# Expert results added in a PSUM bank, row shifts on ScalarE, and expert scatters through two tables

## What is computed

```python
h = h + _L0_attn_ref(_layernorm(h), ...)   # a state-space block with a scan over time
h = h + _L0_ffn_ref(_layernorm(h), ...)    # 8 experts, each takes the 1024 tokens of highest share
h = h + _L1_attn_ref(_layernorm(h), ...)   # windows of 64 tokens; per token, attention among 8 heads
h = h + _L1_ffn_ref(_layernorm(h), ...)    # shared expert + 2 of 8 experts per token, by group
```

```python
output = jnp.zeros_like(x_flat).at[idx.reshape(-1)].add(weighted.reshape(-1, Dd))
```

## Time and profile before

| what | value |
|---|---|
| three runs, median (lowest, highest) | 2762.41 us (2756.27, 2762.47) |
| the profiled execution's own time | 2761.4 us |
| its span, first to last instruction | 2759.4 us |
| VectorE busy | 2382.7 us (86%) |
| TensorE busy | 2294.0 us (83%) |
| GpSimd busy | 2068.2 us (75%) |
| ScalarE busy | 1616.4 us (59%) |

### The profile page before, as it was taken

The page is one execution under the profiler, slowest core; times in us unless marked ns, Lnnn a source line. Parts: engine busy times, 40 slices in busy tenths (PEclk is TensorE's granted clock), DMA queues, the critical chain, the costliest instruction groups (busy, mean ns, idle before and its releaser), DMA issues. The chain is left out here.

```text
span 2759.4 us, 26470 instructions
## 1 busy us (share of the span) xinstructions
PE 2294.0 (83%) x6899; PEld 1098.8 (40%) x6899; DVE 2382.7 (86%) x3555; ACT 1616.4 (59%) x3023; POOL 2068.2 (75%) x1108
## 2 busy tenths in 40 slices
PE   5999999999999999999984148717888888888888
PEld 2444444444444444444432024304444444444444
DVE  3999999999999999999996832226999999999996
ACT  4777777767777777777662124424545555555544
POOL 2889899898898898988992048766777777777772
PEclk8999999999999999999996569857999999999999
DMA  2243333333433333333333013311111111011100
GB/s 75 94 124 99 106 115 105 114 111 93 128 98 108 118 106 110 116 93 115 108 96 98 0 35 73 47 25 31 31 29 30 29 28 31 28 31 31 31 24 23
DMA packets 180609, 199.44 MB, mean 72 GB/s; under 512 B 40062, under 2 KB 170988, under 8 KB 180332
## 3 DMA queue, kind: packets, MB, share of 16 engines
q1 hardware_dynamic: 169196, 189.35, 22.5%
q0 software_dynamic: 11264, 8.40, 2.3%
HBM read 164.44 MB, written 33.25 MB: 72 GB/s over the span
## 5 line engine op out<-in xcount | busy, mean ns | idle before, releaser
L915 POOL TENSOR_TENSOR a_hc<-a_h,a_cs 128x896 f32<-128x896 f32 (+1 forms) x448 | 859.6, 1938 | 55.4 <-DVE a_h L778 54.9
L362 PE MATMUL a_y_bank<-a_hc,a_ident 128*128 128x448 f32 (+1 forms) x1792 | 741.4, 544 | 20.3 <-DVE a_yz L798 19.7
L553 ACT ACTIVATE a_da<-a_dt,a_neg_a 128x448 f32<-128x448 f32 (+1 forms) x896 | 551.8, 631 | 295.6 <-DVE a_h L778 290.6
L778 DVE TENSOR_TENSOR_SCAN a_h<-a_da,a_h,a_dbx 128x448 f32<-128x448 f32 x528 | 583.3, 1135 | 9.5 <-ACT a_da L553 4.4
L362 PEld LDWEIGHTS a_y_bank<-a_hc,a_ident 128*128 128x128 f32 x1792 | 331.6, 190 | 325.2 <-issue 273.0
L2183 POOL TENSOR_TENSOR c_prod<-c_prob,c_qkv 128x1024 f32<-128x1024 f32 x100 | 279.3, 2820 | 189.3 <-DVE c_prob L2053 189.3
L1777 PE MATMUL c_p_E<-c_w_ex,c_hid 128*128 128x512 f32 x800 | 375.4, 599 | 38.3 <-DVE c_sc L2029 36.3
L762 DVE TENSOR_TENSOR a_dbx<-a_dtx,a_b_bank 128x896 f32<-128x896 f32 (+1 forms) x308 | 327.8, 1064 | 15.7 <-PE a_b_bank L355 15.5
L2174 POOL TENSOR_TENSOR c_prod<-c_qkv 128x1024 f32<-128x1024 f32 x100 | 232.7, 2353 | 58.1 <-ACT c_qkv L1845 58.1
L903 POOL TENSOR_TENSOR a_dbp<-a_dtx,a_bs 128x896 f32<-128x896 f32 (+1 forms) x140 | 270.9, 1935 | 0.0
L778 DVE TENSOR_TENSOR_SCAN a_h<-a_da,a_h,a_dbp 128x448 f32<-128x448 f32 x240 | 263.4, 1130 | 0.0
(11 more groups left out here) (306 smaller groups left out, 3744.1 us busy)
## 6 DMA issues: line engine op xcount, KB each, us to landing
a_cs<-c_rows SPq DMA_DIRECT2D x96, 896.0 KB, 5.3
a_bs<-c_rows SPq DMA_DIRECT2D x24, 1120.0 KB, 5.7
a_cs<-c_rows SPq DMA_DIRECT2D x16, 900.0 KB, 4.4
c_x<-h_rows SPq DMA_DIRECT2D x100, 64.0 KB, 2.3
heads<-c_ot SPq DMA_DIRECT2D x25, 256.0 KB, 2.0
c_dealt<-heads SPq DMA_DIRECT2D x200, 32.0 KB, 1.9
rolled<-c_res SPq DMA_DIRECT2D x25, 256.0 KB, 2.4
h_rows<-a_th SPq DMA_DIRECT2D x24, 224.0 KB
```

What stands on the lines that cost most here:

```text
L362: pe.matmul(y_bank[:, d, 0:g.w], ident[:], hc[:, (g.i * NS + n) % HC_RING, d, 0:g.w], start=(n == 0), stop=(n == NS - 1)).then_inc(s_sum, 1)
L553: act.activation(da[:, k % DA_RING, 0:g.w], dt[g.slot][:, d, 0:g.w], ACT.Exp, scale=neg_a[:, d * NS + n:d * NS + n + 1]).then_inc(s_da, 1)
L778: dve.tensor_tensor_scan(h[:, n, d, 0:g.w], da[:, (g.i * 2 * NS + k) % DA_RING, 0:g.w], x, state, ALU.mult, ALU.add).then_inc(s_scan, 1)
L915: pool.tensor_tensor(hc[:, (q.i * NS + n) % HC_RING, :, 0:q.w], h[:, n, :, 0:q.w], cs[:, n % C_RING, 0:q.w].unsqueeze(1).to_broadcast([P, ...
```

## The change

1. Stage C: the experts' parts are no longer summed by two reductions over six slots. VectorE adds them one after another into the shared expert's PSUM bank: `total(c, 0)` adds the attention's rows `h3` to ACC, `total(c, 1)` to `(c, 3)` add a part of 128x512, and `total(c, 4)` writes the result. `keep_acc` goes.
2. The shift of both norms (minus mean times 1/deviation) is computed by ScalarE in four single-column copies behind `rstd`; `less_mean` and `less_mean2` go from VectorE.
3. Banks 1 and 2 of the experts are evicted by VectorE, `by_dve(1)` and `by_dve(2)`, instead of ScalarE.
4. Stage B: there are two tables of rows twice as wide, the norm in the first half and the running sum in the second. Even experts gather and scatter whole rows of table 0, odd ones of table 1, with plain scatters; the addition is done by VectorE in the gathered tile. The second table is filled in stage B: a copy of the norm, and zeros. A gather waits for the scatters of the expert two before.
5. Stage C loads a group from both tables, and GpSimd adds them (`merge`), on which `stats_of` waits.
6. Stage B's TensorE takes the halves of an expert in turn: transposes of a half, then its up-projection.
7. The order of the operations in a turn of stage C is another on all engines.

```diff
 # GpSimd, experts
-        for e in range(XG - 1):
-            gather(e)
+        for e in range(2):
+            gather(e)
         for e in range(E0):
-            if e + XG - 1 < E0:
-                gather(e + XG - 1)
             scatter(e)
+            if e + 2 < E0:
+                gather(e + 2)
...
+            if e == 1:
+                pool.wait_ge(s_second, 16 * SECOND)
+            if e >= 2:
+                pool.wait_ge(s_scatter, 16 * TILES * (e - 1))
...
-                pool.indirect_dma_start(h_rows[:, :], bass.IndirectOffsetOnAxis(ap=index[:, i, e:e + 1], axis=0),
-                                        og[e % 2][:, i, :], None, compute_op=ALU.add).then_inc(s_scatter, 16)
+                pool.indirect_dma_start(tables[e % 2][:, :], bass.IndirectOffsetOnAxis(ap=index[:, i, e:e + 1], axis=0),
+                                        xg[e % XG][:, i, :], None).then_inc(s_scatter, 16)
...
+                    last = dve.scalar_tensor_tensor(out=total, in0=p_t[h][:, i * P:(i + 1) * P], scalar=share[s][:, t:t + 1],
+                                                    in1=total, op0=ALU.mult, op1=ALU.add)
...
+        for b in range(BATCH):
+            span = slice(b * ROWS // BATCH, (b + 1) * ROWS // BATCH)
+            sp.dma_start(tables[1][span, 0:D], tables[0][span, 0:D]).then_inc(s_second, 16)
+        sp.wait_ge(s_fill, 2)
+        for top in range(0, ROWS, P * NZERO):
+            n = min(P * NZERO, ROWS - top)
+            per = NZERO if n == P * NZERO else n // 32
+            sp.dma_start(tables[1][top:top + n, D:2 * D].rearrange("(p k) d -> p k d", k=per),
+                         zeros[0:n // per, 0:per * D].bitcast(F32).rearrange("p (k d) -> p k d", k=per)
+                         ).then_inc(s_second, 16)
```

```diff
 # GpSimd, a turn of stage C
+            def merge():
+                if L is not None:
+                    pool.wait_ge(s_x[L % 3], (L // 3 + 1) * 16 * GT)
+                    pool.wait_ge(s_x2[L % 2], (L // 2 + 1) * 16 * GT)
+                    pool.tensor_tensor(x[L % 3][:], x[L % 3][:], x2[L % 2][:], ALU.add).then_inc(s_merged, 1)
...
             score_products(2)
+            score_products(3)
+            merge()
             add_experts(0)
-            score_products(3)
+            add_experts(1)
             value_products(0)
             value_products(1)
-            add_experts(1)
             add_experts(2)
 # VectorE
         def total(c, k):
+            acc = tile_of("acc", c)[:].rearrange("p (j d) -> p j d", j=GT)
+            if k == 0:
+                result(dve, "acc", c)
+                dve.tensor_tensor(acc, acc, h3[c % SUM_RING][:], ALU.add).then_inc(s_sum, 1)
+                return
+            dve.wait_ge(s_add, c * GT + GT)
+            dve.wait_ge(s_sum, c * EG + k)
+            part = parts[c % 2][:, :, k - 1, :]
+            if k < EG:
+                dve.tensor_tensor(acc, acc, part, ALU.add).then_inc(s_sum, 1)
+                return
...
+            dve.tensor_tensor(res[c % 2][:], acc, part, ALU.add).then_inc(s_free[nth["acc", c][0]], 1)
...
-                    dve.wait_ge(s_x[L % 3], (L // 3 + 1) * 16 * GT)
+                    dve.wait_ge(s_merged, L + 1)
```

More of the change, by code:

```diff
@@ L100, in dram @@
             return debug[name] if name in debug else nc.dram_tensor(name, shape, dt, kind="Internal").ap()
-        h_rows = dram("h_rows", [ROWS, D])
-        n_rows = dram("n_rows", [ROWS, D])
+        tables = [dram(f"rows{k}", [ROWS, 2 * D]) for k in range(2)]
+        n_rows, h_rows = tables[0][:, 0:D], tables[0][:, D:2 * D]
         logits = dram("logits", [E0, NLG])
@@ L1055, in phase_b @@
     w2 = [sb(f"w2{s}", [P, FT, D]) for s in range(2)]
-    xg = [sb(f"xg{s}", [P, TILES, D]) for s in range(XG)]
+    xg = [sb(f"xg{s}", [P, TILES, 2 * D]) for s in range(XG)]
     xw = [sb(f"xw{h}", [P, HT, D]) for h in range(2)]
@@ L1277, in vector @@
             dve.wait_ge(s_share, e + 1)
-            need(dve, s_scatter, 16 * TILES * (e - 1))
             for h in range(2):
                 dve.wait_ge(s_turned, 2 * e + h + 1)
-                dve.tensor_tensor(og[s][:, h * HT:(h + 1) * HT, :], p_t[h][:].rearrange("p (i d) -> p i d", i=HT),
-                                  share[s][:, h * HT:(h + 1) * HT].unsqueeze(2).to_broadcast([P, HT, D]), ALU.mult
-                                  ).then_inc(s_og, 1)
+                for i in range(HT):
+                    t = h * HT + i
+                    total = xg[e % XG][:, t, D:2 * D]
+                    last = dve.scalar_tensor_tensor(out=total, in0=p_t[h][:, i * P:(i + 1) * P], scalar=share[s][:, t:t + 1],
+                                                    in1=total, op0=ALU.mult, op1=ALU.add)
+                last.then_inc(s_og, 1)
     def scalar(act):
@@ L1576, in phase_c @@
     sc = sb("sc", [P, SC_RING, E1, D])
-    parts = [sb(f"parts{s}", [P, GT, SLOTS, D]) for s in range(SUM_RING)]
+    parts = [sb(f"parts{s}", [P, GT, EG, D]) for s in range(2)]
+    h3 = [sb(f"h3{s}", [P, GT, D]) for s in range(SUM_RING)]
     res = [sb(f"res{s}", [P, GT, D]) for s in range(2)]
@@ L1610, in phase_c @@
     s_x = [sem(f"x{s}") for s in range(3)]
+    s_x2 = [sem(f"x2{s}") for s in range(2)]
+    s_merged = sem("merged")
     s_heads, s_dealt, s_res = ([sem(f"{n}{s}") for s in range(2)] for n in ("heads", "dealt", "res"))
@@ L1654, in load @@
                         taken(sp, "proj", L - 3)
[L1655 to L1658, removed]
+                    need(sp, s_merged, L - 1)
+                    for table, tile, done in ((tables[0], x[L % 3], s_x[L % 3]), (tables[1], x2[L % 2], s_x2[L % 2])):
+                        rows = table[L * GW + SHIFT:(L + 1) * GW + SHIFT, D:2 * D].rearrange("(w n) d -> n w d", n=WIN)
+                        for j in range(GT):
+                            sp.dma_start(tile[:, j, :], rows[j * WIN // GT:(j + 1) * WIN // GT]).then_inc(done, 16)
             def store(c):
                 if c is not None and c >= 0:
-                    sp.wait_ge(s_sum, 2 * c + 2)
+                    taken(sp, "acc", c)
                     sp.dma_start(out[c * GW:(c + 1) * GW, :].rearrange("(j p) d -> p j d", p=P), res[c % 2][:]
@@ L1885, in row_scale @@
                     act.activation(rstd[:], lnv[:], ACT.Exp, scale=-0.5).then_inc(s_rstd, 1)
+                    act.wait_ge(s_rstd, L + 1)
+                    for j in range(GT):
+                        i = act.activation(shift[:, j:j + 1], minus[:, j:j + 1], ACT.Copy, scale=rstd[:, j:j + 1])
+                    i.then_inc(s_shift, 1)
             def score_exp():
@@ L1916, in affine @@
                                    bias=cols[:, 2:3]).then_inc(free, 1)
-            def keep_acc():
-                if X is not None:
-                    free = result(act, "acc", X)
-                    need(act, s_sum, 2 * (X - SUM_RING + 1))
-                    act.copy(parts[X % SUM_RING][:, :, OF_ACC, :], tile_of("acc", X)[:].rearrange("p (j d) -> p j d", j=GT)
-                             ).then_inc(free, 1)
             def by_act(n):
@@ L2138, in vector @@
             choose_experts()
-            total_last(0)
+            by_dve(1)
+            hidden(0)
             sum_values(N, 2)
-            hidden(0)
+            total_last(1)
             sum_values(N, 3)
+            total_last(2)
             sum_scores(0)
-            total_last(1)
-            sum_scores(1)
             stats_of()
             hidden(1)
+            total_last(3)
+            sum_scores(1)
+            total_last(4)
             sum_scores(2)
             choose_group()
+            by_dve(2)
+            hidden(2)
             sum_scores(3)
@@ L2152, in vector @@
             add_rows()
+            probs()
             by_dve(4)
-            probs()
-            hidden(2)
-            less_mean2()
             by_dve(5)
-            less_mean()
             hidden(3)
             by_dve(6)
+            sum_values(A, 0)
             by_dve(7)
-            sum_values(A, 0)
+            total_now(0)
             sum_values(A, 1)
-        for k in range(2):
+        for k in range(1, EG + 1):
             total(NG - 1, k)
@@ L2192, in add_experts @@
                     taken(pool, f"ex{2 * j + 1}", X)
-                    need(pool, s_sum, 2 * (X - SUM_RING) + j // 2 + 1)
+                    if X >= 2:
+                        taken(pool, "acc", X - 2)
                     rows = sc[:, n % SC_RING, :, :]
-                    pool.tensor_tensor(parts[X % SUM_RING][:, j, 0:EG, :], rows[:, 0:EG, :], rows[:, EG:E1, :], ALU.add
+                    pool.tensor_tensor(parts[X % 2][:, j, :, :], rows[:, 0:EG, :], rows[:, EG:E1, :], ALU.add
                                        ).then_inc(s_add, 1)
```

115 lines of the change are left out of this document (52 added, 63 removed), and 8 rows, old and new, of the table BANK_ORDER.

## The result

The changed kernel takes 2826.9 us (median of 4 runs, 2825.5 to 2830.2) where the kernel before takes 2762.2 (4 runs): ratio 1.024, 95% interval 1.022 to 1.026. It is slower by 64.7 us; forecast were 2808 us, a range of 2778 to 2848 and 0.87 for slower. In a second comparison the same kernel took 2811.0 beside 2755.1, ratio 1.020 (1.018 to 1.021): 55.9 us slower.

A forecast was written before the change was run, and what follows sets the result against it. VectorE bound the kernel before; the change would close a ring through GpSimd's merge, 37.8 us a turn against 35.1. 2761.4 + 65 (last stage) - 20 (experts) = 2806, rounded up to 2808 us; range 2778 to 2848.

The forecast's parts named there:

- turn 0: Turn 0 of the last stage: 33.9 us against 33.0 before, +0.9 us.
- the drain: End of last stage: two reductions (5.5 us) become four additions (2.7), `shared` covers 1.3 of waits for `dealt`: -4 us.
- the expert stage: Gathers and plain scatters at 1.25 us a step: end at 1800 instead of 1820, -20 us.
- The ring: Each full last-stage turn: GpSimd probabilities to merge 24.15 us, VectorE merge to probabilities 13.45, hand-overs 0.2: 37.8 us.
- VectorE's work: VectorE in a full last-stage turn: 34.9 - 5.5 - 4.5 + 4.2 = 29.1 us, each addition or `by_dve` 0.6.
- The small multiplications: `less_mean` and `less_mean2` leave VectorE's turn: 2.37 and 2.26 us beside a GpSimd product, together some 4.5.
- The early turns: Last-stage turns -3, -2 and -1: +4.7 us, +3.4 (30.2 us) and +6.4 (33.3 us).
- Turn 21: Last-stage turn with no group to load and no merge: 30.4 us against 34.1, -3.7.
- the second rival: Expert stage: the plain scatter costs as much as the accumulating one, +35 us on the forecast, 2843; chance 0.13.
- The second table: Its copy and zeroing, at most 38,500 packets, 60 us on 16 engines, cost nothing; without cover up to 60 us.
- The third rival: Last stage: TensorE or a blocked subtraction lengthens the ring to 38.5 to 39.3 us, 2830; chance 0.12.
- The signs: Value products every 37.8 us, VectorE idle 7 to 9 before statistics, GpSimd's probs wait near 11, last scatter about 1800.

The follow-up runs named there:

- merge twice: Changed kernel with an extra, unused 128x512 addition on GpSimd ahead of the merge: 2843.4 us, ratio 1.031.
- merge in the middle: Changed kernel with GpSimd's merge between score_products(1) and score_products(2): 2701.9 us, ratio 0.980.
- merge first: Changed kernel with GpSimd's merge moved ahead of score_products(0): 2677.0 us, ratio 0.971.
- statistics late: Changed kernel with VectorE's stats_of moved behind sum_scores(3), merge still behind the score products: 2663.2 us, ratio 0.966; once more 2663.9.
- last stage without merge: Kernel before (old tables, expert stage, loads of x) with the changed last stage, no second load and no merge: 2667.0 us, ratio 0.968.
- the experts alone: Kernel before with two tables and plain scatters, old last stage, merge ahead of GpSimd's score products: 2739.9 us, ratio 0.995.
- the experiment: Kernel with merge ahead of score_products(0), with less_mean and less_mean2 back on VectorE in place of ScalarE's shifts: 2724.0 us, ratio 0.988.
- the repeat: The changed kernel itself measured once more, beside the others on one chip: 2811.0 us, ratio 1.020.
- the halves together: Changed kernel with TensorE transposing both halves of an expert before its first product, as before the change: 2815.7 us, ratio 1.022.

## Why the prediction was right

Turns in us, worked out and measured (the first line from the prediction, the others from the expectations):

| kernel | worked out | measured |
|---|---|---|
| changed | 37.8 | 37.7 |
| merge twice | 39.0 | 38.95 |
| merge in the middle | 33.1 | 33.12 |
| merge first | 30.5 to 31.5 | 31.96 |
| statistics late | 31.5 to 33 | 31.15 |
| last stage without merge | 31 to 31.5 | 30.75 |

The mechanism came as forecast. Of its terms two were missed (turn 0 and the drain), and the one of the expert stage was met by errors that offset each other.

- **The ring**: 24.15 us on GpSimd were worked out and 24.12 measured; 13.45 on VectorE and 0.2 of hand-overs, 13.60 measured. That the ring is the cause is shown from both sides: taking the merge or the statistics out of it frees the turn, lengthening it by 1.2 us lengthens the turn by 1.2. The last stage alone gives -88 us and the experts alone -15, together -103, where both with the ring give +56. So the two halves together cost some 159 us more than apart, nearly all of it in the turns: 20 full ones of 37.7 against 30.75 us are 139 us and the first three, 101.4 against 85.5, another 16. The kernel with the late statistics (-93) gets back all but 10 of it: its turn is 0.4 us above 30.75, 24 times.
- **VectorE's work**: additions and `by_dve` at 0.6 us were right (2238.26 to 2238.87). 29.1 us of work a turn was right too: 28.4 busy in the changed kernel, and 31.15 less 1.7 of waits in the one with the late statistics.
- **The small multiplications**: -4.5 us of work. In the changed kernel they would stand behind the probabilities, outside the ring, and by that the gain buys nothing there; this was not run. Where the ring is open the experiment prices it at 47 us. The rule of the Trainium skill, "SBUF — State Buffer", section "Who interferes with whom", fits it again: both multiplications read two tiles in SBUF and take 0.15 us at the least, one of them 2.39 in the median and the other 0.63.
- **The early turns**: -2 and -1 are 30.17 and 33.34 us (30.2 and 33.3 worked out). From the last scatter to the first value product it is +7.7 (8.4). Turn 21 is 30.1 (30.4).
- **Turn 0**: 37.9 us where 33.9 was worked out. I took the score products to run without a gap. In the profile GpSimd waits 3.8 us for two of the copies of qkv:

```profile
1923.93 4.70 POOL L2193 TENSOR_TENSOR c_prod<-c_qkv 128x1024 f32<-128x1024 f32 x2 [0.30 <-ACT c_qkv L1865]
1932.11 2.33 POOL L2193 TENSOR_TENSOR c_prod<-c_qkv 128x1024 f32<-128x1024 f32 x1 [3.47 <-ACT c_qkv L1865]
```

From GpSimd's first value product to `qkv(3)` TensorE takes 20.5 us here (1910.20 to 1930.70) and 19.1 in a full turn (2212.37 to 2231.50): its first twelve matmuls take 4.6 us at a granted clock of 0.55 (1913.8 to 1918.4), the same twelve 2.6 at 1.00 in the full turn (from 2216.48). And GpSimd, with no parts to add between these value products, is ready 2.5 us sooner than in a full turn. The prediction held TensorE against GpSimd in the full turns alone.

- **The drain**: +2.3 us (90.4 against 88.1) where -4 was forecast. The end of the chain that ended last, before and after:

```profile
2739.19 1.98 PE c_p_E L1777 x4
...
2743.56 5.71 PE c_p_E L1777 x14
```
```profile
2799.79 3.78 PE c_p_E L1797 x4
2803.58 0.85 PE c_p_M L1754 x4
2804.43 2.26 PE c_p_E L1797 x4
2806.69 1.78 PE c_p_ACC L1778 x16
...
2808.70 5.71 PE c_p_E L1797 x14
...
2820.27 0.69 DVE c_res L2016
```

From the first of these matmuls to the last ones is 4.4 us before and 8.9 after: `shared` has moved into the last turn's chain (1.78), and the matmuls ahead of it, behind a pause of 3.3 us, run at a granted clock of 0.69 (2795 to 2806), 3.78 us for what took 1.98. I had let `shared` cover a wait for `dealt`; here it is a cost. What lies ahead of these matmuls in the drain is 1.4 us shorter. The additions at the very end saved 0.8 us (from the last matmul's end to the end of the span 10.1 and 9.3), not 2.8: the sum counts four additions, but `total(c, 0)` stands there too (0.7 us), and VectorE waits 0.8 us for GpSimd's last part.
- **The expert stage**: a plain scatter is issued in 0.97 + 0.30 us, as the gather and unlike the accumulating one (1.55 + 0.30), so the second rival is gone. From the first gather to the last scatter the stage takes 187.6 us in the repeat and 185.7 to 189.2 in eight experiments with the same stage; the forecast's sum gives 189.4. Against the 208.6 of before that is -19 to -23, as forecast (-20), but this is partly luck. The profile of before has a late start of VectorE ahead of its first scatter, and the kernel with the new last stage alone, which has the same old expert stage, takes 204.6 without it:

```profile
1643.53 0.69 DVE L1281 TENSOR_TENSOR b_og<-b_p_max,b_share 128x512 f32<-128x512 f32 x1 [9.45 <-remote]
```
```profile
1639.20 1.62 POOL L1400 DMA_INDIRECT h_rows<-b_og,b_index  x1 [0.36 <-DVE b_og L1281]
```

Against 204.6 the repeat gains 17 us, and 6 of these are the halves in turn, which I had at nothing; the tables and the plain scatters gain 11 (193.7 with the halves together). Two errors offset each other in my sum: I kept 34.7 us from the first gather to the first scatter and they are 29.0, and from there to the last scatter it is 158.6, not 154.7.
- **The first profile's expert stage**: it took 201.8 us. This explains 13 of the 19 us by which the measured 64.7 exceeds the forecast's 46; turn 0 and the drain are 10, and the other terms together give 4 back. The rows of that profile:

```profile
1663.88 0.60 PE L1368 MATMUL b_p_tr<-b_ident,b_xg 128*128 128x128 f32 x4
1668.28 5.40 PE L1375 MATMUL b_p_h<-b_xt,b_w 128*128 128x512 f32 x8 [3.81 <-DVE b_xt L1279]
```
```profile
1667.54 0.69 DVE L1279 COPY b_xt<-b_p_tr 128x512 f32<-128x512 f32 x1 [9.15 <-remote]
```

TensorE's transposes end at 1664.5, VectorE's copy of them starts 3.1 us later and TensorE waits 3.8 (0.8 in the repeat). That happens at three experts, and GpSimd's waits for the multiply-adds come to 32.1 us (16.0 in the repeat). What VectorE waited for the profile calls only "remote". No other profile of the new expert stage shows it, and that of before shows it once. The longer time isn't that of the profiled execution alone: all four runs of this comparison took 2825.5 to 2830.2 us, all four of the second 2806.6 to 2812.9. The cause stays open.
- **The second table**: 38,500 packets at most were to be hidden, and are: the DMA share is 0.47 in the 120 us ahead of the gathers (0.10 before), no gather waits for it in the changed kernel's profile.
- **The third rival**, a blocked subtraction: `less_top`'s takes 0.42 us (2208.79), with GpSimd idle beside it. Whether it would block beside a product was not tried. TensorE adds nothing to the ring: the turn is 37.7.
- **The signs**: the merge releases the statistics after 6.9 us of waiting, a little under the 7 to 9 named. GpSimd's wait for the probabilities doesn't stay near 11 us: it was 7.8 before and is 4.4, because `by_dve(2)` now stops GpSimd for 6.7 us ahead of it; the two together are 11.1.

That the repeat's 2811 lies so near 2808 is partly luck: the kernel before took 7 us less in that comparison. In differences it is +56 against +46: turn 0 (4), the drain (6) and some 3 of the expert stage (17 against 20, by the 204.6), less 3 of smaller terms.

**The best version** is the changed kernel with the statistics behind the last score sum: 2663 us, 3.4% under the kernel before and 5.3% under the changed one (0.966 / 1.020 = 0.947).

## What to carry to other kernels

When a wait moves onto an engine that works in order, list what stands behind it there and follow each item until it comes back to the instruction that is awaited. If it comes back, add up the ring and compare it with the turn: the fullest engine's busy time says nothing then, and a microsecond on a member of the ring counts in full, however idle its engine. The cheapest remedy here was not to speed up a member but to move the waiting instruction behind what doesn't need it, or the awaited one ahead. Both halves of a change may be gains and their sum a loss, so time each half alone.

## What the runs showed of the hardware

- Where the ring lets TensorE idle 5.3 us ahead of `up(5)`, the next four matmuls take 3.78 us, and the granted clock in that stretch is 0.50, its lower level of 1.2 GHz; without the pause the same four take 1.96 us at 1.00 (the kernel with the late statistics, 2126.22). The mean over 20 turns falls from 1.00 to 0.91. It costs nothing in the ring, whose members don't wait for TensorE there, but it did cost in the drain and in turn 0.

```profile
2200.00:2204.00 4.00, 3.31 (x4) 1.51 (x5) 4.00 (x6) 0.00 (x0) 0.00 (x0) 0.50 0.01 3
```

- An indirect scatter without accumulation costs GpSimd 1.27 us a step (0.97 and 0.30), with it 1.85.
- An addition of 128x512 floats from PSUM and SBUF into PSUM takes VectorE 0.61 us from start to start (2238.26 to 2238.87).
